# Offset maps in sets by rows of taps, transposed out of PSUM, with the bias in ScalarE's hats; halves turned in two arrangements and a norm out of PSUM

## What is computed

```python
    x = x + _L0_conv_ref(_gn(x), ...)   # three depthwise convolutions with gates, a pooled branch
    x = x + _L1_conv_ref(_gn(x), ...)   # deformable 3 x 3 sampling
    x = x + _L2_conv_ref(_gn(x))        # graph attention over all nodes
    x = x + _L3_conv_ref(_gn(x), ...)   # binary 3 x 3 convolution
```

```python
    # L1: om has, for each of 8 groups, 27 maps: y and x offsets and a mask for each of 9 taps
    om = om_in @ om_w.T + om_b
    off = om[..., :2 * K]; mask = om[..., 2 * K:]
    py = y + dy + off[..., 0]; px = x + dx + off[..., 1]
    sampled = the four neighbours of (py, px) in value, weighted bilinearly
    out = einsum('nhwgk,nhwgkc->nhwgc', mask, sampled) @ op_w.T
    # L2: X holds the nodes, 64 channels each; A joins neighbours in the images and each node to itself
    nrm = max(sqrt(sum(X * X, axis=1)), 1e-8)
    sim = X @ X.T / (nrm[:, None] * nrm[None, :])
    m = (A + sim) * 0.5
    d = exp(diagonal(m) - logsumexp(m, axis=1)); out = relu(X * d[:, None])
```

## Time and profile before

| | us |
|---|---|
| median of 3 runs | 332.7 (331.63 to 333.59) |
| the profiled execution's own time | 331.46 |
| its span, first to last instruction | 329.3 |
| TensorE busy | 289.9 (88%) |
| VectorE busy | 279.0 (85%) |
| ScalarE busy | 160.6 (49%) |
| GpSimd busy | 111.0 (34%) |

### The profile page before, as it was taken

One profiled execution on the slowest core, in us unless ns is written; L12 is line 12 of the kernel. 1 busy time (PEld: TensorE's weight loads), 2 busy tenths in 40 slices (PEclk: granted clock), 3 DMA queues, 4 the chain that ended last, 5 costly groups with the idle time before them and its releaser, 6 DMA issues.

```text
span 329.3 us, 6056 instructions
## 1 busy us (share of the span) xinstructions
PE 289.9 (88%) x2270; PEld 175.4 (53%) x2270; DVE 279.0 (85%) x419; ACT 160.6 (49%) x262; POOL 111.0 (34%) x129
## 2 busy tenths in 40 slices
PE   8698999589699998999998975698888899999796
PEld 8336987237544435566654622594333344358772
DVE  5799999997778699999985758784999999998873
ACT  1499552115345769200000000788898888999200
POOL 4005998811700259999994024000000000000000
PEclk9799999899999999999999999769999999999999
DMA  3421000000000000000000000433000000000503
GB/s 114 144 75 32 15 11 0 2 1 0 3 0 0 0 0 2 2 0 2 2 2 0 2 3 32 159 65 127 1 0 0 0 0 0 0 3 2 117 10 129
DMA packets 7613, 8.72 MB, mean 26 GB/s; under 512 B 2212, under 2 KB 5796, under 8 KB 7588
## 3 DMA queue, kind: packets, MB, share of 16 engines
q1 hardware_dynamic: 6260, 7.20, 7.0%
q10 hardware_dynamic: 1328, 1.18, 1.7%
HBM read 4.18 MB, written 2.10 MB: 19 GB/s over the span
## 4 chain that ended last, share of the span: by engine, by line
PE 45%; POOL 15%; DVE 13%; issue 12%; ACT 9%; ACTq 3%; DMA 1%; DVEq 0%; POOLq 0%
PE ps L1244 12%; POOL arena L558 11%; PE ps L1498 9%; PE ps L1257 8%; PE ps L1381 3%; POOL arena L546 3%; ACT arena L799 3%; PE ps L1567 3%; PE ps L1478 3%; ACT arena L782 2%; PE ps L1278 2%; POOL turns L558 2%; ACTq L347 2%; PE ps L1395 2%; PE ps L1269 1%
## 5 line engine op out<-in xcount | busy, mean ns | idle before, releaser
L1498 PE MATMUL ps<-arena 128*128 (+1 forms) x256 | 63.6, 380 | 6.7 <-ACT arena L782 5.9
L782 ACT ACTIVATE arena<-ps 128x2048 f32<-128x2048 f32 x32 | 60.1, 1878 | 8.3 <-PE ps L1498 8.3
L1498 PEld LDWEIGHTS ps<-arena 128*128 (+1 forms) x256 | 24.3, 97 | 41.5 <-issue 15.3
L1125 DVE TENSOR_TENSOR arena<-arena 128x1024 f32 (+3 forms) x34 | 36.9, 1154 | 4.7 <-ACT arena L782 4.4
L616 ACT ACTIVATE rstd<-mv,eps 128x2 f32<-128x2 f32 x6 | 1.8, 296 | 77.6 <-DVE mv L848 73.4
L558 POOL TENSOR_TENSOR arena<-arena 128x768 f32<-128x768 f32 x21 | 37.7, 1824 | 0.2
L1278 PE MATMUL ps<-ident 128*128 128x128 f32 x262 | 34.4, 295 | 3.3 <-DVE arena L1169 1.7
L1244 PE MATMUL ps<-turns,k 128*128 128x512 f32 x80 | 34.7, 593 | 2.1 <-DVE turns L1076 2.1
L1066 DVE TENSOR_TENSOR turns<-arena,ps 128x1024 f32<-128x1024 f32 x30 | 35.2, 1216 | 1.3 <-PE ps L1395 1.3
L1278 PEld LDWEIGHTS ps<-ident 128*128 128x128 f32 x262 | 33.5, 210 | 4.4 <-DVE arena L1169 1.9
L1257 PE MATMUL ps<-arena 64*64 64x240 f32 (+3 forms) x576 | 29.7, 361 | 4.1 <-issue 2.6
(11 more groups left out here) (232 smaller groups left out, 493.7 us busy)
## 6 DMA issues: line engine op xcount, KB each, us to landing
scratch_x<-xs SPq DMA_DIRECT2D x4, 256.0 KB
arena<-arena SPq DMA_DIRECT2D x2, 512.0 KB, 3.3
out<-arena SPq DMA_DIRECT2D x4, 256.0 KB, 2.4
sN<-in_bias_n SPq DMA_DIRECT2D x48, 0.0 KB
xs<-in_x SPq DMA_DIRECT2D x8, 64.0 KB
xs<-in_x ACTq DMA_DIRECT2D x8, 64.0 KB
arena<-arena SPq DMA_DIRECT2D x4, 128.0 KB, 3.1
arena<-arena ACTq DMA_DIRECT2D x4, 128.0 KB, 3.5
```

Source lines behind the costliest of these rows:

```text
L782: act.activation(E[k], ps[:, (k % 2) * 2048:(k % 2 + 1) * 2048], ACT.Exp, scale=0.5 / SPLIT ** 2, accum_out=rowsum[:, bass.ds(i, 1)]).then ...
L1125: dve.tensor_tensor(out=cc, in0=cc, in1=E[k][:, lo * P:hi * P], op=ALU.add).then_inc(sem(name), 1)
L1498: ins = pe.matmul(bank(b0 + q), w, m[:, bass.ds(i * P + 512 * q, 512)], start=(t == 0), stop=(t == 1 and q > 0))
```

## The change

Maps are made in sets by rows of taps: set order is y, mask, x for the taps of dy = 0, then of dy = 2, then dy = 1. The products write to PSUM as before; VectorE transposes straight from PSUM to `omX`, with no eviction. The bias is then one column per map (`map_bias`, `minus_bias`, built once by VectorE from eight DMAs in place of 48) and ScalarE adds it in the activations that make the hats, one activation per tap. All hats are ScalarE's, positive now, so the output is added. GpSimd's masks and folds come in another order, and its weight building has 28 + 48 products in place of 2 + 40. After the window TensorE puts the residual of the first half into PSUM in front of the output product; VectorE takes moments from there, ScalarE normalizes from there and keeps the sum. Squares and sums are taken half by half; the second half is added into `xs` by VectorE as before, with moments of 256 columns each. The halves `hm` have the pattern high, low, high: two arrangements HM and MH are turned (64 transposes) in place of three. The diff, cut to its core:

```diff
 # layout of the maps, helpers (new)
+        MAP_ROWS = (0, 2, 1)
+        Y, MASK, X = range(3)
+        def given(kind, tap):
+            return TAPS * kind + tap
+        def place(kind, tap):
+            return TAPS * MAP_ROWS.index(tap // 3) + 3 * kind + tap % 3
+        def one_map(kind, tap):
+            return omX[:, place(kind, tap) * PX:(place(kind, tap) + 1) * PX]
+        def maps_bank(js, h, s):
+            return (4, 0)[js % 2] + 2 * h + s
-        hm = cut(10240, 4096).bitcast(F16)
+        hm = cut(10240, 3072).bitcast(F16)
-        HM = cut(14336, 2048).bitcast(F16)
-        HH = cut(16384, 3072).bitcast(F16)
-        MM = cut(19456, 3072).bitcast(F16)
+        HM = cut(14336, 3072).bitcast(F16)
+        MH = cut(17408, 3072).bitcast(F16)
 # SyncE
-            sp.wait_ge(sem("bias_in"), 16)
-            for js, lo, n in swapped_maps:
-                for m in range(lo, lo + 2 * n, 2):
-                    for c4 in range(C4):
-                        sp.dma_start(view(sN, 3 + 2 * js, [(1, 2)], 32 * c4 + 4 * m, 4),
...
+            for swap, t in enumerate(bias_rows):
+                for c4 in range(C4):
+                    sp.dma_start(t[32 * c4:32 * c4 + 32, :], dram(bias_n, (c4 ^ (2 * swap)) * 104, [(0, 32), (1, 104)])
+                                 ).then_inc(sem("map_bias_in"), 16)
-            sp.wait_ge(sem("x2_ready"), 4)
+            sp.wait_ge(sem("x2_ready"), 2)
+            sp.wait_ge(sem("x2_kept"), 2)
 # GpSimd: weights of the maps
-                pool.tensor_tensor(out=view(k1, c * 1280, [(4, 256), (1, 4)]), in0=view(raw1, c * 320, [(1, 256), (0, 4)]),
...
-            for js, lo, n in swapped_maps:
-                for c in range(2):
-                    for s in range(2):
+            for c in range(2):
+                for j, o, n in map_runs:
+                    last = pool.tensor_tensor(
+                        out=view(k1, c * 1280 + 2 * (j // 8) * P + 4 * (j % 8), [(32, 8), (4, n), (1, 4)]),
...
+            link(last)
+            for kind in (Y, MASK, X):
+                for tap in SWAPPED:
+                    for c in range(2):
                         for half in range(2):
...
+            last.then_inc(sem("k1_maps"), 1)
 # GpSimd: masks and folds
-            for hat in range(3):
-                mask_hats(hat, 0)
-            pool.wait_ge(sem("fold_first"), 1)
-            pool.wait_ge(sem("maps_turned"), 12)
-            mask_hats(2, 2)
-            for hat in (0, 2, 1):
-                mask_hats(hat, 1)
-            pool.wait_ge(sem("hats_x"), 3)
-            fold_row(1)
-            pool.wait_ge(sem("over"), 1)
-            fold_row(2)
-            mask_hats(1, 2)
-            fold_row(3)
-            mask_hats(0, 2)
-            fold_row(4)
+            pool.wait_ge(sem("mask_biased"), 1)
+            for n, hat in enumerate((0, 2, 1)):
+                pool.wait_ge(sem("hats_y"), n + 1)
+                mask_hats(hat, 0)
+            pool.wait_ge(sem("hats_x"), 1)
+            fold_rows(2)
+            for n, hat in enumerate((2, 0, 1)):
+                pool.wait_ge(sem("hats_y"), n + 4)
+                mask_hats(hat, 2)
+            pool.wait_ge(sem("hats_x"), 2)
+            fold_rows(1)
+            pool.wait_ge(sem("hats_y"), 7)
+            mask_hats(0, 1)
+            pool.wait_ge(sem("over"), 1)
+            pool.wait_ge(sem("hats_x"), 3)
+            fold_rows(3)
+            mask_hats(2, 1)
+            fold_rows(4, 5)
+            mask_hats(1, 1)
+            fold_rows(6, 7, 8)
 # ScalarE: maps
-            evacuate(0, 0)
...
-            hats_x(2)
+            def below(t, kind, taps):
+                for tap in taps:
+                    ins = act.activation(tap_map(t, tap), one_map(kind, tap), ACT.Relu, scale=-1.0,
+                                         bias=bias_col(minus_bias, kind, tap))
+                return ins
...
+            def size_of(t, kind, taps):
+                for tap in taps:
+                    act.activation(tap_map(t, tap), one_map(kind, tap), ACT.Abs,
+                                   bias=bias_col(map_bias, kind, tap)).then_inc(sem("sizes"), 1)
...
+            def row_y(dy, first, second):
+                taps = range(3 * dy, 3 * dy + 3)
+                first(hy, Y, taps).then_inc(sem("hats_y"), 1)
+                bias_masks(dy)
+                second(hy, Y, taps).then_inc(sem("hats_y"), 1)
+                size_of(sizes_y, Y, taps)
+                rest_of_one(hy1, sizes_y, dy).then_inc(sem("hats_y"), 1)
+            act.wait_ge(sem("maps_turned"), 4)
+            row_y(0, below, above)
+            hats_x((0, 1))
+            act.wait_ge(sem("maps_turned"), 8)
+            hats_x((2,))
+            rest_of_x(0)
+            row_y(2, above, below)
...
+            row_y(1, below, above)
+            act.wait_ge(sem("maps_turned"), 16)
+            hats_x((3, 4, 5))
+            rest_of_x(1)
 # ScalarE: after the window
+            keep_sum(0)
+            root(rstd[:, 0:2], view(mv, 1, [(2, 2)]))
+            act.wait_ge(sem("shift2"), 1)
+            for j in range(2):
+                act.activation(view(xh2, j * 512, [(PX, 2), (1, PX)]), view(bank(4), j * PX, [(512, 2), (1, PX)]), ACT.Identity,
+                               bias=shift2[:, j:j + 1], scale=rstd[:, j:j + 1]).then_inc(sem("xhat2"), 1)
+            keep_sum(1)
+            squares(0, 0)
+            squares(0, 1)
+            root(rstd[:, 2:4], view(mv, 5, [(2, 2)]))
+            squares(0, 2)
+            squares(0, 3)
             for q in range(4):
+                squares(1, q)
+            keep_nodes(0)
+            root(rs, n2, add_eps=False)
+            keep_nodes(1)
+            for q in range(4):
+                act.wait_ge(sem("xx"), q + 1)
+                act.activation(view(hm, q * 1536, [(192, 8), (128, 2), (1, 64)]), view(xx, q * 512, [(64, 8), (0, 2), (1, 64)]),
+                               ACT.Copy).then_inc(sem("h_half"), 1)
+                if q in (1, 2):
+                    keep_nodes(q + 1)
+            for q in range(3):
+                act.wait_ge(sem("turn_done"), 2 * q + 1)
+                act.activation(view(HM, q * P, [(4 * P, 8), (1, P)]), view(turned(q, 0), 0, [(P, 8), (1, P)]),
+                               ACT.Copy).then_inc(sem("HM"), 1)
 # VectorE: maps
-            def turn_maps(js, nqs=range(NQ)):
-                    dve.transpose(cols(omX, 8 * js * PX, PX, nq), to_rows_in(omN[js % 2], nq)).then_inc(sem("maps_turned"), 1)
+            def turn_maps(js, h):
+                for nq in (2 * h, 2 * h + 1):
+                    dve.wait_ge(sem("maps_done"), 4 * js + 2 * h + 2)
+                    b = maps_bank(js, h, 0)
+                    dve.transpose(cols(omX, 8 * js * PX, PX, nq), view(bank(b), (nq % 2) * PX, [(HW, HW), (512, C2), (1, HW)])
+                                  ).then_inc(sem("maps_turned"), 1)
+            turn_maps(0, 0)
+            turn_maps(0, 1)
+            turn_maps(1, 0)
+            turn_maps(1, 1)
+            turn_maps(2, 0)
...
             dve.tensor_tensor(out=view(folds[0], 0, [(3 * PX, 3), (PX, 3), (1, PX)]),
...
+            turn_maps(2, 1)
+            turn_maps(3, 0)
+            turn_maps(3, 1)
 # VectorE: after the window, first half
+            for s in range(2):
+                dve.wait_ge(sem("op_done"), s + 1)
+                for j in range(2):
+                    m = 2 * j + s
+                    dve.bn_stats(stats[:, 6 * m:6 * m + 6], bank(4 + s)[:, j * PX:(j + 1) * PX]).then_inc(sem("sum_moments"), 1)
...
+            scaled_nodes(0)
+            scaled_nodes(1)
+            scaled_nodes(2)
+            low_half(0)
+            scaled_nodes(3)
+            low_half(1)
+            low_half(2)
+            keep_turned(MH, 0, 1, "MH")
+            low_half(3)
+            for q in range(1, 4):
+                keep_turned(MH, q, 1, "MH")
+            keep_turned(HM, 3, 0, "HM")
 # TensorE
+            for s in range(2):
+                pe.matmul(bank(4 + s), ident, view(xs, s * PX, [(512, 2), (1, PX)]), start=True, stop=False)
             for h in range(2):
                 pe.wait_ge(sem("window_turned"), 2 * h + 2)
                 for s in range(2):
-                    pointwise(bank(4 + 2 * h + s), k2, 2, s, oN, h, "op_done")
+                    pointwise(bank(4 + 2 * h + s), k2, 2, s, oN, h, "op_done", begun=(h == 0))
-                for which in range(3):
+                for which in range(2):
                     for j in range(8):
                         ins = pe.transpose(view(turned(q, which), P * j, [(1, P)]),
-                                           view(hm, (8 * q + j) * 256 + 64 * which, [(1, P)]), ident16)
+                                           view(hm, (8 * q + j) * 192 + 64 * which, [(1, P)]), ident16)
-                    for t, m in enumerate((HH, MM)):
+                    for t, m in enumerate((HM, MH)):
```

368 lines of the change are left out of this document (186 added, 182 removed).

## The result

| | before | after |
|---|---|---|
| median, us (runs) | 333.14 (331.63 to 334.53, 4) | 321.25 (319.56 to 323.36, 4) |
| profiled execution, us | 331.46 | 320.82 |
| its span, us | 329.3 | 319.0 |
| its mean granted TensorE clock | 0.974 | 0.973 |

The ratio is 0.9647, with a 95% interval of 0.9574 to 0.972. Measured a second time, beside other kernels, it was 0.9696 (0.9638 to 0.9754). By the medians the change saves 11.9 and 10.6 us; I had forecast 8.1 (324.6 us, range 321.4 to 328.4). The second median, 321.46 us, lies just inside the range.

The account below looks back on a forecast made before the run. TensorE bounds the maps, VectorE then TensorE the window loop, a dependent chain the stretch to the spans. +0.7 - 2.5 - 1.5 - 4.8 = -8.1 us gives 323.4 profiled, 324.6 median; eight-in-ten range 321.4 to 328.4.

Parts of the forecast that it names:

- Front, +0.7: GpSimd's longer weight building moves its casts beside VectorE's normalization at 75 to 80 us: +0.7 us, bounds 0 and two 1.4 us waits.
- Rival 5: GpSimd's casts miss the normalization, loop starts at 123.1, turning at full clock from the first block: 322.6 us; 0.50 together with forecast.
- Maps, -2.5: Map stage: no evictions, fold done earlier, only two transposes behind the last product; first window product 2.5 us earlier.
- nearest by source: Map transposes from PSUM priced at 0.68 us like the four already reading PSUM; 1.06 kept as bound for strided writes.
- Tap operations 0.36 apart: ScalarE's hats made tap by tap, 256-element operations starting every 0.36 us; x hats done at 133.2 us.
- Folds, -1.5: Window loop: GpSimd's folds end at 169.1 us, so TensorE's stall for them goes, saving 1.5 us (between 1.1 and 2.0).
- Normalization, -2.7: Loop end to scaling: moments in PSUM, ScalarE normalizing the first half; scaling starts at 208.55 instead of 211.29 us.
- rival 4: Moments in PSUM and ScalarE's normalization hand over too often, nothing won up to the scaling: 327.1 us; chance 0.13.
- Halves, -2.3: Scaling to first span: 64 blocks turned instead of 96, fewer ScalarE copies; 10.2 us in place of 12.53.
- Spans, 0: Spans behind the turning are unchanged work, two matmuls of the same width per 512 columns: no gain.
- Rival 2: TensorE's half clock reaches from the turning into the spans, costing 1.5 to 2.5 us: 326.6 us; chance 0.15.

Follow-up runs that it names:

- everything together: Changed kernel with 11 unused TensorE products ahead of the depthwise convolution, 12 more ahead of the turning, and TensorE's span loop written out: 317.47 us, ratio 0.9549.
- both fillings and the rolled loop: Changed kernel with 11 unused TensorE products ahead of the depthwise convolution and 12 more ahead of the halves' turning, span loop kept rolled: 318.7 us, ratio 0.9583.
- the second execution: Second profiled execution of the changed kernel, nothing altered, measured beside other kernels: span 318.9 us; median of that session 321.46 us, ratio 0.9696.

## Why the prediction fell short

The direction and the places were right; the sum was short by 3.8 us (2.5 against the second median), and the range ended at 321.4, 0.15 us above the result. The runs of one kernel differ by more than that 0.15, so on which side of the edge the median fell is chance; the steps below are not. By the steps of the sum:

- **Front, +0.7: the step that failed, and in sign.** I had added up GpSimd's instructions and asked only where its casts would land. They landed at 70.8 to 73.4 us and met nothing: the 48 small products took 12.9 us, 0.27 each and not 0.37, and the last cast of identS 0.30 us and not 1.41. With the convolution at the same clock, that stage took as long as before (+0.1). What I removed without a price were two products of 1.89 us ahead of GpSimd's others. They had pushed those beside VectorE's products, on the path: 1.1 us by the trace, 1.6 when put back. Rival 5 had the first half of this (casts that meet nothing), none of the second.
- **Maps, -2.5: right in size, for a wrong reason in part.** The transposes took the bound of 1.06 and not the 0.68 that I had taken as nearest. The last two begin at 122.28 us, behind the last product, and the first window product 1.85 us later; the forecast had left 1.8. The choice "nearest by source" was wrong: the side that counts is the one with columns in SBUF.
- **Tap operations 0.36 apart: 0.40.** My row had a PSUM source, these read SBUF. The estimate from the Trainium skill, "VectorE: DVE Perf Modes", section on the TRN2 errata, was right (0.40), as its estimate is for the row with PSUM (0.36). Its dearer PSUM source for VectorE is not seen here: 0.71 us from both. The x hats came 3.4 us later than I said (136.6), and GpSimd still finished before it was asked.
- **Folds, -1.5: -1.1.** The stall is gone: no matmul waits for a fold. The loop takes 64.92 to 64.95 us instead of 66.02 in every kernel that has the new maps.
- **Normalization, -2.7: -3.2.** It is 15.95 to 15.97 us in seven profiled executions. In two others (16.45 and 16.20, with GpSimd's products put back and with everything together) the clock fell during the last transposes to nodes. The moments taken in PSUM and ScalarE's half of the work do what the diff says; rival 4 falls.
- **Halves, -2.3: -3.5 in the profiled execution.** The mis-sized term is the clock: I let the half clock last as long as before. In five executions with the new halves it covered about 3 us (9.05 to 9.40 us for the stage), in one 6 us (10.54), and in four none (8.85; three of them with the filling there, one without). In three of these four it had come a little earlier, between 200 and 207 us, over transposes to nodes and unused products; only the execution with both fillings and the rolled loop shows none there. At equal clock, the new halves give 2.5 us (11.31 to 8.85) at full and 2.0 (12.53 to 10.54) at half, so the work term was right. Why the half clock mostly lasts shorter with 64 transposes than with 96 was not found.
- **Spans, 0: -1.15.** "Unchanged work" was true of the matmuls. It was not true of the rolled loop around them, with one tile fewer to address, which I never looked at. Rival 2 looked for the clock there, and the clock was full.
- **Not the change's: the depthwise convolution (+1.5) and the tail (+0.6).** Both differ between executions of one kernel. The kernel before was profiled in an execution with the convolution at full clock, which can account for the 1.24 us between that execution and the median.

In the second execution, which is like the kernel before's in the convolution, the stages are -0.9 (front), +0.1, -2.5, -1.1, -3.2, -3.1 and -1.15, in all -11.8 against the forecast -8.1; the tail then takes 1.4 us more, so the span is 10.4 us shorter. Of the 3.7 us missing up to the far products the two stages of the front are 1.5, normalization and halves are 1.5 and the spans 1.15, less 0.4 for the folds.

## What to carry to other kernels

Price an instruction that is removed by what its going moves, too: two large GpSimd products cost little where they stood, and held the next ones back until they ran beside VectorE's products on the path. For a form that the trace lacks, find which side of the access sets the cost before choosing the nearest row; here the layout in SBUF, not the source memory. And when a tile disappears from a rolled loop, look at the loop's period too, and not at the matmuls alone: where two engines hand over to each other every 2 us, written-out code gave 1.3 us more for one changed line.

## What was new about the hardware

- A VectorE transpose of 128x512 fp32 costs 0.71 us, and 1.06 as soon as either side walks SBUF in steps of 4 elements; the same steps in PSUM are free. The Trainium skill, "SBUF — State Buffer", section "Specifications (TRN2)", gives SBUF lines of 16 bytes with a price for each change of line, which fits the one side; PSUM's are shorter there, and these transposes don't feel it.
- TensorE's clock fell to its lower level after the same idle time (2.6 us) in six of nine executions, and in none of the four in which eleven unused products filled it; the fall cost 1.5 to 1.7 us.
- TensorE's rolled loop with three addressed tiles takes 4.43 us for two spans, with two tiles 4.33, written out 4.21 (69.7, 68.56 and 67.27 us over the 32 spans, 24 of them in the loop).
